# Attention on one core: four of the ten sums of exp tiles per unit moved to accumulating DMA, three denominator groups for six, units written out without a loop

## The reference

```python
q = (x @ Wq.T).reshape(b, t, h_kv, g, d).transpose(0, 2, 3, 1, 4)   # t = 2048, h_kv = 8, g = 4, d = 32
k = (x @ Wk.T).reshape(b, t, h_kv, d).transpose(0, 2, 1, 3)
v = (x @ Wv.T).reshape(b, t, h_kv, d).transpose(0, 2, 1, 3)
att = jnp.einsum('bhgqd,bhkd->bhgqk', q, k) / scale
att = jax.nn.softmax(att, axis=-1)
y = jnp.einsum('bhgqk,bhkd->bhgqd', att, v)
```

## Time and profile before

| what | us |
|---|---|
| median of three runs | 3699.42 |
| the profiled execution, whole | 3694.73 |
| its span | 3693.0 |
| PE busy in the span | 3572.8 |
| DVE, ACT, POOL busy | 2233.6, 1597.7, 1631.6 |
| attention | about 430 to 2160 of the span |

### The profile page before, as it was taken

One profiled execution on the slowest core, in us unless ns is written; L12 is line 12 of the kernel. 1 busy time (PEld: TensorE's weight loads), 2 busy tenths in 40 slices (PEclk: granted clock), 3 DMA queues, 4 the chain that ended last, 5 costly groups with the idle time before them and its releaser, 6 DMA issues. The chain is left out here.

```text
span 3693.0 us, 54945 instructions
## 1 busy us (share of the span) xinstructions
PE 3572.8 (97%) x17964; PEld 2347.2 (64%) x17964; DVE 2233.6 (60%) x3725; ACT 1597.7 (43%) x2990; POOL 1631.6 (44%) x604
## 2 busy tenths in 40 slices
PE   6998999999999999999999989799999999999999
PEld 4777455554545545555455448688888888887787
DVE  5542877776777777777777548644444444443627
ACT  3210266665666656666666643222222222213544
POOL 1111388887988888888888830000000000000010
PEclk8999799999999999999999999899999999999999
DMA  6662211111011111110100025621111111113222
GB/s 225 197 188 90 76 36 31 33 28 39 22 30 37 29 35 25 33 30 25 41 22 19 10 93 178 195 73 29 28 37 32 29 28 29 28 41 115 83 70 83
DMA packets 177698, 228.37 MB, mean 62 GB/s; under 512 B 39680, under 2 KB 120832, under 8 KB 173632
## 3 DMA queue, kind: packets, MB, share of 16 engines
q1 hardware_dynamic: 156496, 154.69, 14.9%
q0 software_dynamic: 18672, 68.70, 5.8%
q10 hardware_dynamic: 2304, 2.10, 0.2%
HBM read 162.13 MB, written 62.78 MB: 61 GB/s over the span
## 5 line engine op out<-in xcount | busy, mean ns | idle before, releaser
L748 DVE TENSOR_REDUCE att_chunk_max<-att_scores 128x1 f32<-128x512 f32 x2048 | 1269.7, 683 | 435.7 <-PE att_scores L819 433.5
L729 ACT ACTIVATE att_exp<-att_scores_T 128x512 f32<-128x512 f32 x2048 | 1046.7, 603 | 597.5 <-PE att_scores_T L833 585.1
L685 POOL TENSOR_TENSOR att_exp_pair<-att_exp 128x2048 f32<-128x2048 f32 x256 | 1168.5, 4580 | 271.8 <-ACT att_exp L729 271.7
L819 PE MATMUL att_scores<-att_k_stack,att_q_stack 96*128 96x512 f32 x2048 | 874.2, 449 | 17.1 <-DMA att_q_stack<-q_scratch 13.3
L833 PE MATMUL att_scores_T<-att_q_stack,att_k_stack 98*128 98x512 f32 x2048 | 748.2, 403 | 9.4 <-issue 6.7
L819 PEld LDWEIGHTS att_scores<-att_k_stack,att_q_stack 96*128 96x128 f32 x2048 | 393.1, 192 | 419.3 <-DVE att_chunk_max L748 204.5
L844 PE MATMUL att_y_acc<-att_exp,att_v_head 128*32 128x512 f32 x4096 | 496.3, 602 | 0.0
L833 PEld LDWEIGHTS att_scores_T<-att_q_stack,att_k_stack 98*128 98x128 f32 x2048 | 387.0, 189 | 159.0 <-ACT att_exp L729 64.6
L1206 POOL DMA_DIRECT2D inter_scratch<-gu_inter x84 | 45.4, 540 | 883.1 <-DVE gu_inter L1149 883.1
L703 POOL TENSOR_TENSOR att_exp_pair<-att_exp_pair 128x2048 f32<-128x2048 f32 x64 | 293.7, 4589 | 2.6
L1260 ACT ACTIVATE gu_magnitude<-gu_value 128x512 f32<-128x512 f32 x88 | 55.9, 635 | 516.7 <-DVE gu_value L1291 516.7
(11 more groups left out here) (190 smaller groups left out, 4847.1 us busy)
## 6 DMA issues: line engine op xcount, KB each, us to landing
att_q_stack<-q_scratch SPq DMA_DIRECT2D x96, 256.0 KB, 5.0
shared_raw<-in_wd_t POOLq DMA_DIRECT2D x34, 256.0 KB, 3.0
qkv_x_tile<-in_x SPq DMA_DIRECT2D x16, 512.0 KB, 4.8
q_scratch<-qkv_qk_out_hi POOLq DMA_DIRECT2D x32, 256.0 KB, 3.2
q_scratch<-qkv_qk_out_lo POOLq DMA_DIRECT2D x32, 256.0 KB, 4.3
qkv_wqkv_raw<-in_wmod POOLq DMA_DIRECT2D x8, 1024.0 KB, 7.5
qkv_wmod<-in_wmod POOLq DMA_DIRECT2D x8, 1024.0 KB, 8.1
y_scratch<-att_y_out SPq DMA_DIRECT2D x32, 256.0 KB, 2.4
```

The lines of the kernel that those rows point to most:

```text
L685: nc.gpsimd.tensor_tensor(ps[PAIR_SLOT[j]][:], pr[2 * j % NP][:], pr[(2 * j + 1) % NP][:], ALU.add).then_inc(pair_done, 1)
L729: nc.scalar.activation(pr[k % NP][:, h * NB:(h + 1) * NB], stp[bank(u, c, GH * k + h)][:], ACT.Exp, scale=INV_SQRT_DH).then_inc(exp_done, 1)
L748: nc.vector.reduce_max(cmax[c % 2][:, q:q + 1], turn_buffer(u, c, q)[:], AX.X).then_inc(sm_done, steps_done(u, q))
L819: nc.tensor.matmul(turn_buffer(u, c, q)[:], qs[c % 4][0:SR, h, qt * P:(qt + 1) * P], ks[c // QB % 2][0:SR, kc * NB:(kc + 1) * NB], start=T ...
```

## The change

POOL has nine sums a unit in place of ten: the eight pairs, and one sum of two quads (`oct_sum`). Between them four DMAs, issued by POOL, add one 1 MB `exp_pair` buffer onto another (`sum_by_dma`, a DMA with `accum_op`): after pairs 1, 3, 5 and 7. Two of these replace POOL's two quad sums, the other two sum pairs 4 and 5 and pairs 6 and 7, which were not summed before. (So a unit has thirteen sums of exp tiles, nine on POOL and four by DMA, where it had ten, all on POOL.) What is left for PE are three groups: the sum of pairs 0 to 3, of pairs 4 and 5, and of pairs 6 and 7, at k = 0, 2 and 6 of the next unit (DEN_AT). The copy of the denominator moves from k = 4 to 6, the reciprocal from k = 8 to 9, `y_out` from after pair 3 to after pair 4. The loop over units is gone: all 32 units are written out, and every wait compares with a constant.

```diff
@@ -465,16 +465,18 @@
     NST = 3
     TQ = 6
     NP, NS = 8, 5
-    PAIRS, QUADS = KT // 2, 2
-    ND = QUADS + PAIRS - 2 * QUADS
+    PAIRS = KT // 2
     PAIR_SLOT = (0, 1, 2, 3, 4, 1, 3, 2)
-    DEN_SLOT = (0, 2, 4, 1, 3, 2)
-    DEN_AHEAD = (10, 12, 14)
-    DEN_LATE = (0, 2, 4)
+    DMA_AFTER = (1, 3, 5, 7)
+    DMA_SUM = ((0, 1), (2, 3), (4, 1), (3, 2))
+    OCT_AFTER = 5
+    DEN_SLOT = (0, 4, 3)
+    ND = len(DEN_SLOT)
+    DEN_AT = (0, 2, 6)
     RP = 8
-    DEN_COPY = 4
-    RECIP_AT = 8
-    Y_AFTER = 3
+    DEN_COPY = 6
+    RECIP_AT = 9
+    Y_AFTER = 4
     DW = GH * NB // P
     TSTEP = 14
     PER = NTURN // KT
@@ -513,7 +515,8 @@
         sm_ready, sm_done = sem("scores_ready"), sem("scores_consumed")
         mT_hi, m_stored = sem("max_T_hi"), sem("max_rows_stored")
         pv_done, pair_done, den_done = sem("pv_done"), sem("pair_done"), sem("den_done")
-        quad_done = sem("quad_done")
+        oct_done = sem("oct_sum_done")
+        dma_sum = [sem(f"dma_sum_done{i}") for i in range(len(DMA_SUM))]
         y_copied, y_done, y_stored = sem("y_copied"), sem("y_done"), sem("y_stored")
         const_done = sem("consts_done")
         den_copied, den_stored, den_loaded = sem("den_copied"), sem("den_stored"), sem("den_loaded")
@@ -524,7 +527,6 @@
 
 
         BODY = 2 * QB
-        LOOPS = (NU - 1) // BODY
         NX = GH * KT
 
         def order(u, c):
@@ -548,11 +550,7 @@
         def units(eng, unit):
 
 
-            unit(0, 0, 0)
-            with eng.Fori(0, LOOPS) as it:
-                for j in range(BODY):
-                    unit(it * BODY + (1 + j), (1 + j) % BODY, it * (BODY // QB) + (1 + j) // QB)
-            for u in range(1 + LOOPS * BODY, NU):
+            for u in range(NU):
                 unit(u, u % BODY, u // QB)
 
         def is_first(u):
@@ -676,14 +674,36 @@
             def pair(u, j):
                 pool.wait_ge(exp_done, NST + 2 * GH * (j + 1) + u * NX)
 
-                if j in (0, 1, 2):
-                    pool.wait_ge(den_done, (1, 4, 6)[j] + u * ND)
-                elif j == PAIRS - 1:
-                    pool.wait_ge(den_done, ND + 2 + u * ND)
-                elif j in (5, 6):
-                    pool.wait_ge(quad_done, j - 4 + u * QUADS)
+                if j == 0:
+                    pool.wait_ge(den_done, 1 + u * ND)
+                elif j == 1:
+                    if u:
+                        pool.wait_ge(dma_sum[2], u * 16)
+                elif j == 2:
+                    if u:
+                        pool.wait_ge(dma_sum[3], u * 16)
+                elif j == 3:
+                    pool.wait_ge(den_done, 3 + u * ND)
+                elif j == 4:
+                    pool.wait_ge(den_done, 2 + u * ND)
+                elif j == 5:
+                    pool.wait_ge(dma_sum[0], 16 + u * 16)
+                elif j == 6:
+                    pool.wait_ge(dma_sum[1], 16 + u * 16)
+                elif j == 7:
+                    pool.wait_ge(oct_done, 1 + u)
                 nc.gpsimd.tensor_tensor(ps[PAIR_SLOT[j]][:], pr[2 * j % NP][:], pr[(2 * j + 1) % NP][:],
                                         ALU.add).then_inc(pair_done, 1)
+
+            def sum_by_dma(u, i):
+                into, other = DMA_SUM[i]
+                pool.wait_ge(pair_done, NP // 2 + DMA_AFTER[i] + 1 + u * PAIRS)
+                pool.dma_start(ps[into][:], ps[other][:], accum_op=ALU.add).then_inc(dma_sum[i], 16)
+
+            def oct_sum(u):
+                pool.wait_ge(dma_sum[0], 16 + u * 16)
+                pool.wait_ge(dma_sum[1], 16 + u * 16)
+                nc.gpsimd.tensor_tensor(ps[0][:], ps[0][:], ps[2][:], ALU.add).then_inc(oct_done, 1)
 
             def y_out(u, c):
 
@@ -697,10 +717,10 @@
                     pair(u, j)
                     if j == Y_AFTER and not is_first(u):
                         y_out(u - 1, c - 1)
-                    if j % 2 == 1 and j < 2 * QUADS:
-                        pool.wait_ge(pair_done, NP // 2 + j + 1 + u * PAIRS)
-                        first = ps[PAIR_SLOT[j - 1]]
-                        nc.gpsimd.tensor_tensor(first[:], first[:], ps[PAIR_SLOT[j]][:], ALU.add).then_inc(quad_done, 1)
+                    if j in DMA_AFTER:
+                        sum_by_dma(u, DMA_AFTER.index(j))
+                    if j == OCT_AFTER:
+                        oct_sum(u)
 
             pool.sem_inc(pair_done, NP // 2)
             units(pool, unit)
@@ -847,12 +867,11 @@
 
             def denominators(u, i):
 
-                if i < QUADS:
-                    pe.wait_ge(quad_done, i + 1 + u * QUADS)
+                if i == 0:
+                    pe.wait_ge(oct_done, 1 + u)
+                    pe.wait_ge(den_copied, u + 1)
                 else:
-                    pe.wait_ge(pair_done, NP // 2 + QUADS + i + 1 + u * PAIRS)
-                if i == 0:
-                    pe.wait_ge(den_copied, u + 1)
+                    pe.wait_ge(dma_sum[i + 1], 16 + u * 16)
                 part = ps[DEN_SLOT[i]]
                 for h in range(GH):
                     ins = nc.tensor.matmul(dp[h * DH:(h + 1) * DH, :], ones[:], part[:, h * NB:(h + 1) * NB],
@@ -887,10 +906,8 @@
                                 by_v(u, c, g, k - b)
                             elif not is_first(u):
                                 by_v(u - 1, (c - 1) % BODY, g, KT - b)
-                        if k in DEN_AHEAD:
-                            denominators(u, DEN_AHEAD.index(k))
-                        if k in DEN_LATE and not is_first(u):
-                            denominators(u - 1, len(DEN_AHEAD) + DEN_LATE.index(k))
+                        if k in DEN_AT and not is_first(u):
+                            denominators(u - 1, DEN_AT.index(k))
                     ahead_turn()
                     scores_t(u, c, k, 3)
                     if transposing:
@@ -908,7 +925,7 @@
             units(pe, unit)
             for b in (2, 1):
                 by_v(NU - 1, (NU - 1) % BODY, HKV - 1, KT - b)
-            for i in range(len(DEN_AHEAD), ND):
+            for i in range(ND):
                 denominators(NU - 1, i)
```

## The result

The change makes the kernel slower: 3748.56 us (median of four runs, 3738.31 to 3765.06) against 3699.52 before. The ratio is 1.0136, with a 95% interval of 1.0111 to 1.0161. The forecast was 3621, with a range up to 3695. The profiled execution is the longest of the four, 3765.06 us, with a span of 3763.4, 70 us above that of before.

A forecast was written before the change was run, and what follows sets the result against it. PE was taken to bound the kernel. From 3694.7 us, -79 (groups), -11 (loop), +3 (end of attention) and +9 (stores) gave 3617; with the median 4.7 above the profiled run, 3621, range 3598 to 3695.

The forecast's parts named there:

- the one on the maxima's stores: Unit's end: low store has 0.9 us of room before the next first scores_T; slight collision with third accumulation, +9 us.
- POOL to be late by over 10 us: POOL's sums: eight exp tiles in the ring let POOL run over 10 us late before ACT feels it.
- Rival A: Unit's end: accumulations hold up the maxima's stores; landing of 8.6 us gives 3792 us, slower from 5.6 on; chance 0.13.
- Fewer groups: PE in attention: 93 denominator groups fewer at 0.85 us each, -79 us; a unit becomes 51.5 us.
- The loop: Unit loop written out: its two returns, costing 6.0 and 5.1 us, go; -11 us.
- POOL's capacity: POOL per unit: nine sums and y's product 42.5 us, four DMA issues at 0.54 each, in all 44.7 of 51.5.
- L: Time an accumulating 1 MB DMA takes to land: taken as 7 us, between 6.9 and 16.2.
- B: Accumulations take over 12.6 us, so POOL's quads' sum and PE at k = 6 wait; 3739 us at 16.2; chance 0.08.
- C: POOL becomes the bound through its DMA issues, at 4 us each 58.5 us a unit, 3830 us; chance 0.04.
- E: Sums arrive late only in units loading new k and v, one in four: 8 x 3 us, 3645 us; chance 0.08.
- D: PE gives back half: work hidden behind the groups surfaces, a group's going brings 0.4 us, 3660 us; chance 0.10.
- the end of attention: Unit 31, paced by POOL: pair 7 ends 3.9 us sooner, last denominator waits 7 for a DMA; together +3 us.

The follow-up runs named there:

- the last version: Changed kernel with the third accumulation issued behind the sum of quads and the denominator group that reads it moved from k = 2 to k = 4: 3621.54 us, ratio 0.9787.

## Why the prediction was wrong

**The step that failed** is the one on the maxima's stores: "I take 0.3 us x 31 = 9". It came to 89.9 us of waiting and about 53 of slow clock. The latter is read beside the last version above, which has the same instructions and not this wait: PE is busy for 3547.9 us against 3495.1. Together they are 143 of the 144 us between the two profiled executions (3765.06 and 3621.38). Three things in the step were off.

- *When the third accumulation is issued.* The step had it 4.2 us ahead of the low store (44.5 and 48.7). In a unit that starts undisturbed it is 1.1 ahead (682.39 and 683.52). The 3.1 us between are y's product on POOL, which stands ahead of pair 5 and so of that accumulation: it waits 3.1 us for the rows of the denominator, which are loaded beside the second accumulation and take 5.0 us in place of 2.0. With y's product behind the issue the lead was 3.9 us. The prediction had no term for this overlap, and allowed POOL to be late by over 10 us; but POOL's time also sets when a transfer starts.
- *Until when a small store waits.* The low store landing at the accumulation's end was taken as the worst case, 0.5 us into the unit, with a lead of 4.2 us. With a lead of 3.9 us, in the first unit, PE waits 0.7 us, which is close to it. With the leads of 0.8 to 1.2 us that 19 units have, the low store still lands about when the accumulation does, and PE waits 3.75 us and more. A transfer without an add does the same, and another queue doesn't help. The trace of before had a price in the earlier trace rows, 8.6 us for 1.7. The prediction argued that more had been on its way there.
- *What a wait costs.* It was priced at its length. The trace of before could have told otherwise, at the loop's return: 3.38 us idle, then 5.9 us at a clock of 0.53, and the return cost 6.0 us. I read only the sum, and put it down to the loop.

```profile
902.80:906.18 3.38, 0.03 (x1) 0.01 (x1) 1.02 (x2) 0.60 (x1) 2.56 (x1) 0.80 0.50 116
906.18:912.07 5.89, 5.89 (x22) 2.58 (x26) 2.08 (x3) 1.20 (x2) 1.94 (x1) 0.53 0.94 207
```

Rival A named the place and the direction. With a landing of 6.9 us its own formula gives (6.9 - 2.8) x 31 = 127 us, 3739, near the measured 3748.56 by luck: it had no slow clock, and counted 31 full waits where 12 low stores were held up less or not at all. It had a chance of 0.13, and the range ended below it.

**What held.** Fewer groups: units of 51.6 us, where 51.5 were worked out. The loop: 10.5 us for 11. POOL's capacity: nine sums, product and four issues are 45.9 us of 51.6 in the last version (44.7 worked out; an issue costs 0.87 and not 0.54). L: 6.9 us at least for an accumulation and 4.5 for a copy, as estimated from the rate of the DMA engines and the small landing (6.9 and 4.4); by the two pages of the Trainium skill cited in the prediction the estimate was 6.8. B, C and E did not occur, nor D.

**What agrees by luck.** The version without the collision measures 3621.54 us, and the sum gave 3621. But the sum holds 9 us for the stores, which this version doesn't pay, and only 3 us for the end of attention. From the last copy of y before unit 31's to the last denominator group it was 52.5 us before and is 64.3 in this version (2019.88 to 2084.17): 12 us more. Pair 7 ends 60.7 us after the unit's start, where 52.3 were worked out. In the changed kernel the same stretch is 65.1 us. So a second term of the sum was too small by 9 us, and the 9 us for the stores happened to cover it. Nor does a version whose third accumulation is issued later make the forecast of this kernel right.

**What stays open.** By what rule the DMA engines share themselves. In the changed kernel a low store 0.11 us or less behind an accumulation's issue lands undisturbed, one 0.24 to 0.55 behind is held up in part, one 0.78 behind almost to the end, while the high store 0.6 behind lands 2.5 us before the end. These leads came about by themselves; no run set them. Why the rows of the denominator land about 1 us later in some units, so that y's product waits 4.1 us and more, was not followed. Nor was it followed why a wait of 2.06 us left the clock full where one of 1.13 us didn't.

## What to carry to other kernels

A large transfer added to idle DMA engines is not free for the small ones that PE waits for: look for each small store or load that lands with little room, and order the large one's issue behind it. Price a wait of the bounding matmul engine from a place in the trace where it has idled, with the clock of the stretch behind it, not by the wait's length. An engine with time to spare still sets when the DMAs behind its instructions start.

## What the runs showed of the hardware

- An 8 KB store issued 0.78 to 1.22 us after a 1 MB accumulation, as the second of two, lands after 6.5 to 8.0 us in place of 1.9, from SP's queue and from ACT's; issued 3.9 us after it, after 3.7 us (4.5 with a 256 KB store just ahead of it); up to 0.11 us after it, after 1.9 (from ACT's queue once 3.2). The first of the two lands after 5.2 us in the median. Behind a plain 1 MB copy the second lands after 4.3 us.
- An accumulating DMA of 1 MB within SBUF lands after 6.9 us at least (median 7.0 to 7.8 in these kernels), a plain one after 4.5; POOL is held 0.87 and 0.60 us by their issues.
- PE waits of 2.2 to 5.0 us at a unit's start were each followed by 3 to 7 us at half clock, with accumulations in the kernel and without. Of shorter ones, waits of 1.13 and 1.41 us brought it too, waits of 0.59 and of 2.06 us did not. A DMA share of 0.98 without a longer wait did not either.
- A sum on POOL that starts before an accumulation's issue has ended takes 4.86 us in place of 4.58: the sum of quads behind the third issue, and 4.59 where that issue comes after it.
